# A decoder layer with experts, last stage: three of a token's six expert results summed on TensorE, three on VectorE

## The reference, cut to what matters

```python
x = _layernorm(x + _L0_ffn_ref(x, ...), axis=-1)

def _L0_ffn_ref(...):
    probs = jax.nn.softmax(router_logits, axis=-1)
    topk_w, topk_idx = jax.lax.top_k(probs, K)                      # K = 6
    topk_w = topk_w / jnp.sum(topk_w, axis=-1, keepdims=True)
    ...
    h = jax.nn.silu(jnp.einsum('th,eih->tei', x, experts_w1))
    y = jnp.einsum('tei,ehi->teh', h, experts_w2)
    routed_out = jnp.einsum('teh,te->th', y, combine)               # six weighted rows per token
    return (routed_out + shared_out).reshape(orig_shape)
```

## Time and profile before

| | us |
|---|---|
| median of three executions | 1401.5 (1398.18 to 1402.94) |
| the profiled execution, its time | 1399.86 |
| its span, first to last instruction | 1398.0 |
| last stage, first addition to the last aggregate | 1291.1 to 1387.1 |

### The profile page before, as it was taken

The page is one execution under the profiler, slowest core; times in us unless marked ns, Lnnn a source line. Parts: engine busy times, 40 slices in busy tenths (PEclk is TensorE's granted clock), DMA queues, the critical chain, the costliest instruction groups (busy, mean ns, idle before and its releaser), DMA issues.

```text
span 1398.0 us, 32488 instructions
## 1 busy us (share of the span) xinstructions
PE 1016.2 (73%) x9108; PEld 867.2 (62%) x9108; DVE 785.7 (56%) x2447; ACT 416.3 (30%) x1061; POOL 565.1 (40%) x780
## 2 busy tenths in 40 slices
PE   5699999977776777677765498889888888885000
PEld 4588887867675667566764376678676766673000
DVE  5477777754444444444443365556555555552996
ACT  3355555533232323232321022222222222221121
POOL 0122222221454545454546034456444545553454
PEclk9899999987888878887877589999999999997555
DMA  6455555530221212121132065567555555642994
GB/s 204 146 173 171 171 175 182 180 91 24 76 70 67 70 66 70 66 70 66 67 97 102 24 183 163 166 199 215 179 173 176 184 167 181 195 145 101 300 315 170
DMA packets 136190, 197.13 MB, mean 141 GB/s; under 512 B 18397, under 2 KB 111062, under 8 KB 136152
## 3 DMA queue, kind: packets, MB, share of 16 engines
q1 hardware_dynamic: 68200, 104.04, 24.3%
q10 hardware_dynamic: 47920, 41.09, 10.4%
q0 software_dynamic: 20032, 51.55, 10.1%
HBM read 105.76 MB, written 95.03 MB: 144 GB/s over the span
## 4 chain that ended last, share of the span: by engine, by line
PE 53%; another core or an unknown queue 16%; issue 10%; ACT 7%; DVE 6%; ACTq 4%; DMA 1%; POOL 1%; DVEq 1%; SPq 0%; POOLq 0%
PE psum L746 7%; PE psum L769 7%; PE psum L534 5%; PE psum L718 4%; PE psum L750 4%; PE psum L763 3%; PE psum L779 3%; PE psum L593 3%; PE psum L523 2%; PE psum L547 2%; PE psum L649 2%; PE psum L558 2%; ACTq L969 2%; PE psum L690 1%
## 5 line engine op out<-in xcount | busy, mean ns | idle before, releaser
L1082 POOL DMA_INDIRECT expert_results<-arena,udest x224 | 237.8, 1062 | 278.9 <-issue 227.8
L1064 POOL DMA_INDIRECT expert_rows<-row,dest x192 | 186.9, 973 | 69.1 <-issue 67.9
L1461 DVE COPY arena<-arena 128x896 f32 x224 | 129.4, 640 | 90.1 <-PE psum L750 63.1
L746 PE MATMUL psum<-arena 128*128 128x256 f32 x448 | 129.2, 438 | 60.7 <-ACT arena L983 49.6
L746 PEld LDWEIGHTS psum<-arena 128*128 128x128 f32 x448 | 92.0, 216 | 80.5 <-ACT arena L983 54.0
L1443 DVE COPY arena<-psum 128x512 f32<-128x512 f32 x112 | 72.1, 686 | 82.0 <-remote 45.4
L769 PE MATMUL psum<-arena 128*128 128x128 f32 x896 | 117.5, 285 | 0.0
L769 PEld LDWEIGHTS psum<-arena 128*128 128x128 f32 x896 | 106.7, 195 | 9.9 <-issue 9.9
L1035 POOL TENSOR_TENSOR xnb<-xn,c_bout 128x256 f32<-128x256 f32 x32 | 23.3, 727 | 219.8 <-DVE ln_r L1167 207.7
L690 PE MATMUL psum<-c_wgate,x2t 128*128 128x64 f32 x128 | 28.6, 364 | 107.0 <-ACT x2t L920 98.9
L974 ACT ACTIVATE arena<-psum 128x512 f32<-128x512 f32 x56 | 33.5, 597 | 237.4 <-PE psum L750 160.5
(11 more groups left out here) (204 smaller groups left out, 2188.8 us busy)
## 6 DMA issues: line engine op xcount, KB each, us to landing
expert_rows<-zeros SPq DMA_DIRECT2D x64, 536.0 KB, 4.8
arena<-expert_rows ACTq DMA_DIRECT2D x224, 134.0 KB
arena<-in_w_experts SPq DMA_DIRECT2D x64, 448.0 KB
arena<-expert_results SPq DMA_DIRECT2D x32, 768.0 KB, 5.2
xn<-in_x SPq DMA_DIRECT2D x32, 128.0 KB, 2.1
cbt<-in_ctx_t SPq DMA_DIRECT2D x32, 128.0 KB, 4.7
cn<-in_ctx SPq DMA_DIRECT2D x32, 128.0 KB
xt<-in_x_t ACTq DMA_DIRECT2D x30, 128.0 KB, 4.7
```

Source lines behind the costliest of these rows:

```text
L746: pe.matmul(ps_uy[:, v, :], uhm[:, 4 * u + v, :], uw[:, 4 * u + v, 2 * (IM + IQ) + D:UW], start=True, stop=False)
L1064: pool.indirect_dma_start(listd, bass.IndirectOffsetOnAxis(ap=dest[u][:, j:j + 1], axis=0), row[u][:], None).then_inc(sem(f"scatter{u}"), 16)
L1082: pool.indirect_dma_start(yd, bass.IndirectOffsetOnAxis(ap=udest[u][:, v:v + 1], axis=0), uy[:, 4 * u + v, :], None, bounds_check=T * K - ...
L1461: dve.tensor_copy(uw[:, 4 * u + v, :], ring[:, bass.ds(e & (WS - 1), 1), :].rearrange("p a n -> p (a n)"))\
```

## The change

The six weighted rows of a token are divided. Rows 3, 4 and 5 stay on VectorE as before (`add_slot(3)` now starts from `xall`). Rows 0, 1 and 2 go to TensorE: ScalarE multiplies the identity by the tokens' weights, one activation per row (`scale_ident`), which gives three diagonal matrices in `scaled`, two buffers in free space of `arena`; TensorE multiplies each with its rows of `y6` and accumulates the three products in PSUM (`e_sum`), in one of two banks; VectorE adds this to its own sum (`add_sum`), which now raises `ln3_sum`. On ScalarE the scalings of tile s are called in step s, ahead of `apply3` and `store_e`, which now lag by two. Loads, GpSimd's work and the statistics are the same.

```diff
+ON_PE = 3
...
+        scaled = [arena[:, NT * 2 * P + b * ON_PE * P:NT * 2 * P + (b + 1) * ON_PE * P].rearrange("p (k n) -> p k n", k=ON_PE)
+                  for b in range(2)]
...
+        ps_e = [psum[:, i, 0:D] for i in range(2)]
...
+            def e_sum(k, u):
+                t = 4 * k + u
+                pe.wait_ge(*ld("y6_ld", k, u))
+                pe.wait_ge(*ev("scaled_done", t))
+                pe.wait_ge(*ev("ln3_sum", t - 2))
+                for j in range(ON_PE):
+                    q = pe.matmul(ps_e[u % 2], scaled[u % 2][:, j, :], y6[u][:, j, :], start=j == 0, stop=j == ON_PE - 1)
+                q.then_inc(sem("e_ready"), 1)
+
+            tiles(pe, [(0, e_sum)], ways=4)
...
+            def scale_ident(k, u):
+                t = 4 * k + u
+                act.wait_ge(*ev("e_ready", t - 2))
+                for j in range(ON_PE):
+                    q = act.activation(scaled[u % 2][:, j, :], ident[:], ACT.Copy, scale=weights[:, bass.ds(t, 1), j:j + 1]
+                                       .rearrange("p a k -> p (a k)"))
+                q.then_inc(sem("scaled_done"), 1)
+
...
-            tiles(act, [(0, apply3), (0, store_e)], ways=4)
+            tiles(act, [(0, scale_ident), (2, apply3), (2, store_e)], ways=4)
...
-                    if j == 0:
+                    if j == ON_PE:
                         dve.wait_ge(*ld("y6_ld", k, u))
                         dve.wait_ge(*ev("ln3_done", t - 4))
                     else:
-                        dve.wait_ge(sem(f"e_chain{u % 2}"), (K - 1) * (2 * k + u // 2) + j)
+                        dve.wait_ge(*half("slots_done", t, 0) if j > ON_PE + 1 else ev("slot_done", t))
...
+            def add_sum(k, u):
+                t = 4 * k + u
+                r = ln["ln3", u][0]
+                dve.wait_ge(*ev("e_ready", t))
+                dve.wait_ge(*ev("slots_done", t))
+                dve.tensor_tensor(r[:], ps_e[u % 2], r[:], ALU.add).then_inc(sem("ln3_sum"), 1)
...
-            tiles(dve, [(2, sums3), (0, add_slot(0)), (1, add_slot(3)), (2, mean3), (0, add_slot(1)), (1, add_slot(4)),
-                        (0, add_slot(2)), (1, add_slot(5))], ways=4)
+            tiles(dve, [(2, sums3), (0, add_slot(ON_PE)), (1, add_sum), (0, add_slot(ON_PE + 1)), (2, mean3), (0, add_slot(ON_PE + 2))], ways=4)
```

More of the change, by code:

```diff
@@ L61 @@
 PAGE = ("need", "start", "filled", "beyond", "taken", "base", "place", "moved", "top")
-PER_TILE = {"pt_ready": 2, "pt_evac": 2, "w_copied": 4, "h_ready": 2, "page_steps": len(PAGE)}
+PER_TILE = {"pt_ready": 2, "pt_evac": 2, "w_copied": 4, "h_ready": 2, "page_steps": len(PAGE), "slots_done": 2}
 IM = 128
@@ L504, in _ @@
                    "cr_ready", "x2t_ready", "lg_ready", "gu_ready", "rank_ready", "sd_ready",
-                   "ux_ready", "h_ready", "y_ready")
+                   "ux_ready", "h_ready", "y_ready", "e_ready")
             pe.wait_ge(sem("first_consts"), n_first)
@@ L789, in _ @@
             credit(act, "v_evac", "ln1_done", "gn_done", "ln2_done", "ln3_done", "q_evac", "exp_done", "pt_evac", "ot_evac", "xbt_evac", "z_evac", "w_evac", "yt_done",
-                   "x2t_evac", "lg_evac", "ntop_done", "wexp_done", "tope_done", "th_done",
+                   "x2t_evac", "lg_evac", "ntop_done", "wexp_done", "tope_done", "th_done", "scaled_done",
                    "silu_done", "y_evac")
@@ L1108, in _ @@
                    "rank_read", "dest_done", "sg_done", "sh_done", "xsh_done", "xb_kept", "a_kept", "ux_evac", "w_copied",
-                   "udest_done", "uplace_done", "uplaces_done", "ln3_sum", "ln3_stat", "ln3_mv")
+                   "udest_done", "uplace_done", "uplaces_done", "slot_done", "slots_done", "ln3_sum", "ln3_stat", "ln3_mv")
             dve.wait_ge(sem("first_consts"), n_first)
@@ L1488, in stage @@
                     else:
-                        dve.wait_ge(sem(f"e_chain{u % 2}"), (K - 1) * (2 * k + u // 2) + j)
+                        dve.wait_ge(*half("slots_done", t, 0) if j > ON_PE + 1 else ev("slot_done", t))
                     dve.scalar_tensor_tensor(r[:], y6[u][:, j, :], weights[:, bass.ds(t, 1), j:j + 1]
-                                             .rearrange("p a k -> p (a k)"), r[:] if j else slot(xall, t),
+                                             .rearrange("p a k -> p (a k)"), slot(xall, t) if j == ON_PE else r[:],
                                              ALU.mult, ALU.add)\
-                       .then_inc(sem(f"e_chain{u % 2}" if j < K - 1 else "ln3_sum"), 1)
+                       .then_inc(sem("slot_done" if j == ON_PE else "slots_done"), 1)
                 return stage
+            def add_sum(k, u):
[4 more added lines that the diff above has]
+                dve.tensor_tensor(r[:], ps_e[u % 2], r[:], ALU.add).then_inc(sem("ln3_sum"), 1)
             def sums3(k, u):
```

## The result

The changed kernel takes 1410.8 us, the median of 20 executions (1392.5 to 1423.7), against 1396.3 for the kernel before, measured beside it (20 executions, 1380.5 to 1409.2). The ratio is 1.0077, with a 95% interval of 1.0048 to 1.0105: slower by 0.8%, 10.8 us. The medians stand 14.5 us apart; the ratio leaves out executions more than 1.5% above the fastest of their kernel, and that is more of the changed kernel's. Two later comparisons, each on one chip for both kernels, gave 1.0174 (1.0076 to 1.0272) and 1.0109 (1.0055 to 1.0163).

A forecast was written before the change was run, and what follows sets the result against it. VectorE was taken to pace the last stage, and after the change a loop of waits through ScalarE. 1311.2 us plus 15 ways round, 3 at full clock and the rest at half, gave 1425 us, range 1406 to 1433.

The forecast's parts named there:

- the loop: Last stage: aggregate, GpSimd, activation, store, scalings, matmuls, PSUM addition; two tiles need one way round, 6.54 or 7.84 us.
- the clock: TensorE in the last stage: pauses keep it mostly at half clock, 3 of 15 ways round at full.
- rival 1: Full clock is kept in the last stage: 1409 us (1404 to 1418), chance 0.27.
- the sum: Whole time: first load, first matmuls, 15 ways round, last tile's end and time outside, to 1425 us.
- 15 X: Last stage, PSUM addition of tile 1 to that of tile 31: 15 ways round the loop, two tiles each.
- The bound before: Last stage of the kernel before: VectorE sets the pace, 9.88 of 10 us busy, transfers close behind.
- X at full clock: One way round the loop for two tiles, matmuls at 1.56 us: 6.54 us, 3.27 a tile.
- X at half clock: One way round the loop for two tiles, matmuls at 2.86 us: 7.84 us, 3.92 a tile.
- rival 2: Last stage faster, VectorE's work decides with transfers right behind: 17 us given back, 1383 us, chance 0.04.
- my formula: Whole time as 1311.2 us plus 15 ways round: 1409.3 all at full clock, 1428.8 all at half.
- At no cost: Last stage: first scalings lie before the first load, later loads are never late, new waits and buffer cost nothing.
- The signs that I named: Last stage after: VectorE busy a quarter less, waiting 1.3 or 1.9 us a tile; DMA share under 0.93; clock 0.5 to 0.7.

The follow-up runs named there:

- e2: Changed kernel with ScalarE's activation and store three steps behind the scalings instead of two: stage 84.7 us, ratio 0.9954 to the kernel before.
- e12: Changed kernel with activation and store three steps behind the scalings, repeated on another chip: stage 84.3 us, ratio 0.9875 to the kernel before.
- e1: The changed kernel again without edit, for a second trace and comparison: stage 117.7 us, ratio 1.0174 to the kernel before.
- e6: Changed kernel with only the first of each tile's three matmuls, all scalings kept: stage 103.7 us, ratio 1.0062 to the kernel before.
- e9: The changed kernel once more without edit, for a third trace: stage 115.0 us, ratio 1.0109 to the kernel before.
- e4: Changed kernel with 24 unused matmuls put in front of TensorE's last stage: stage 123.3 us in one trace, no ratio.
- e7: Changed kernel with two spare matmuls behind each tile's three: stage 111.9 us, ratio 1.0099 to the kernel before.
- e10: Changed kernel with a lag of four and every load cut in halves, issued earlier: stage 77.6 us, ratio 0.9846 to the kernel before.

## Why the prediction was off

It forecast slower by 25 us (1399.9 to 1425), 1.8%. The sign and the loop held; the clock in the loop didn't, and with it the size. The ratio says 10.8 us, the medians 14.5, the stages of the two traces 16.7. The 1410.8 measured lie inside the range of 1406 to 1433, but in the part that rival 1 had lent it, so that is luck for the forecast and no support for its clock.

Of the sum only 15 X was off. From the first addition to the PSUM addition of tile 1 the changed kernel took 5.1 us (1272.37 to 1277.50; 5.6 predicted), from there to that of tile 31 106.0 (1383.50; 15 X was 113.7), and from there to the last store's issue 3.9 (1387.41; 4.0).

- **The bound before**: right. VectorE paced it, 98.3 and 98.8 us.
- **The loop**: right, shown by e2 and e12: one number changed in ScalarE's order takes 31 to 33 us out of the stage. That alone decides against the sum of VectorE's work (2.01 us a tile), which would have said 28 us faster.
- **X at full clock**: predicted 6.54, measured 6.59. By terms: aggregate to activation 1.79 (I took 1.95; it lay between the bounds of 1.62 and 2.09, on the side to which "GPSIMD Engine Reference", section "Specifications", of the Trainium skill pointed); activation to end of store issue 1.12 (1.11); to the first scaling 0.21 (0.05, an estimate from no row, and above my upper bound of 0.15); scalings 0.99 (1.00); handovers 0.05 and 0.13 (0.04 each); matmuls 1.56 (1.56); PSUM addition and addition 0.74 (0.79). A single scaling took 0.386 us. An estimate by "ScalarE: Activation LUTs", section "Rules for kernel authors", of the Trainium skill is 0.41, which agrees. To lay three of them end to end, 1.22, was the prediction's own step, and that doesn't agree: they overlap and took 0.99.
- **X at half clock**: predicted 7.84, measured 7.95. The sum rests on these two lengths. The 2.93 us a tile for the kernel before, on which the prediction's 5.86 and the 17 us of rival 2 rest, stands in none of its rows, which give 2.89 and 3.00.
- **A term was missing**: the last row of the timeline above. Once in four tiles ScalarE stood for 1.14 us before the scalings, with nothing to wait for ("issue"), where it stands 0.72 otherwise. That is where the program's loop over four tiles goes round. The kernel before has the same loop; there ScalarE was idle for some 2.3 us before every activation, which would hide such a pause, and now ScalarE is on the path. TensorE's starts show it: 1331.97, 1338.56, 1345.67, steps of 6.59 and 7.11. In seven rounds that is 3 to 3.6 us. That the loop's end is the cause is read from the place and the period alone; no run took it away.
- **The step that failed: the clock.** I gave 3 of 15 ways round at full clock and 12 at half. The reason was the earlier trace rows: work with pauses at half clock, 2.60 of 3.40 us, hadn't lifted the clock there. In the loop it did:

```profile
1308.60:1312.60 4.00, 2.81 (x6) 1.85 (x6) 2.12 (x6) 1.58 (x4) 1.27 (x4) 0.50 0.72 248
1312.60:1316.60 4.00, 1.67 (x7) 1.06 (x6) 3.50 (x10) 1.59 (x4) 1.43 (x5) 0.92 0.58 211
```
TensorE had worked 2.92 us at a time with pauses of 0.9 to 1.3 us (the rows at half clock above), and at 1313 the clock rose and stayed full to the last matmul, with TensorE busy 4.55 of 10 us. In e1 it rose out of the same work at 1349. In e6, with 1.22 us of matmuls in every 3.2, it stayed at half from the first to the last tile. So one row of paused work at half clock was no ground for 12 rounds at half. In the changed kernel the half clock lies before 1314: in the first matmuls and, at least in part, in tiles 3 to 10, which are 4 rounds.

By the matmuls: at full clock those of the stage are 32 x 1.56 = 49.9 us, at half 32 x 2.92 = 93.4. Busy were 59.2, 64.8 and 59.0 us, so 21, 34 and 21% of the matmuls ran at half clock, not 80%. With the share measured, my formula gives 1409.3 + 0.21 x 19.5 = 1413.4, 13.5 above before, and with the missing 3 to 3.6 us 16.5 to 17.1; the stage measured 16.7. Why the clock rose where it did, and why it fell again in e1, stays open.
- **Rival 1** (full clock kept, 1409; 1404 to 1418 with up to a third of the loops at half clock) is what came: 1410.8 with 21% at half clock. On the evidence of the earlier trace rows I had it at 0.27. Its full clock isn't sure either: in e1 and e9 it fell within the same steady work.
- **Rival 2** (VectorE's work, transfers behind) came true in the kernels with a lag of three and four, at 84 and 78 us a stage, and not in the changed one.
- **At no cost**: VectorE waited for the first load and 0.4 us for the second, and for none after; the first scalings lay ahead of them. Right.
- **The signs that I named**: VectorE's busy time in the stage fell by 26% (92.88 to 68.73), it waited 21.1 + 19.6 us for the matmuls, 1.3 a tile, and the DMA share fell to 0.72, all as forecast. The granted clock, 0.88 instead of 0.5 to 0.7, was the sign that failed.

What remains open: from what pattern of pauses the clock falls (it did in the first rounds of the changed kernel, late in e1 and e9, again and again in e4, hardly in e7), and how much of the difference between 10.8 and 16.7 us is the spread of the executions. Two repeats at 1.7% and 1.1% lie on the larger side.

## What to carry to other kernels

Before work is moved to an idle engine, write down in what order every engine takes part in it and look for a ring, a chain of waits that comes back to where it began, as the loop of this case. Here the scalings had no need to stand behind the activation, and one digit of lag made 17 us of loss in the stage into 14 us of gain (in the whole time 10.8 us of loss, and 6.5 and 17.5 us of gain). A work count per engine gives only a floor; a ring's time, divided by the tiles it spans, is the other floor, and more lag divides it by more tiles, until something else is the bound, as here with lag four. When several engines show gaps and all waits point in a circle, it is a ring.

## What the runs showed of the hardware

- **A DMA share near 1 isn't the highest rate.** Before, 0.93 went with 296 GB/s; with loads in halves and issued earlier (e10), 1.04 went with 410 GB/s, and over the whole stage 0.94 with 365. The way to tell was to give the loads their buffers earlier and see whether the stage got shorter.
- **TensorE's clock can differ between executions of one kernel** whose work is steady but has pauses: 0.88, 0.81 and 0.87 over the stage in three traces. Two tiles cost 6.6 or 8.0 us by it, so one trace of such a stage is not enough to size it.
- **The clock can rise out of work with pauses.** It rose after matmuls of 2.92 us with pauses of 0.9 to 1.3 us at half clock (changed kernel, e1). It had not risen with TensorE busy for 2.60 of 3.40 us, nor with 1.22 us of matmuls in every 3.2 (e6).
- **Full clock at the start wasn't kept by itself** (e4, one trace: 0.72 over the stage). With spare matmuls behind the real ones it was 0.95 (e7, one trace), and the stage took 111.9 us against 115.0 to 117.7; in the whole time no gain shows (1.0099).
